# Second expert products two steps behind the first, a third gelu buffer, and a small GpSimd write behind each gather and scatter

## What is computed

```python
logits = -dist2 + jnp.einsum('bld,ed->ble', x, rw) + rb
topv, topi = jax.lax.top_k(logits, TOP_K)
w = jax.nn.softmax(topv, axis=-1)
hidden = jax.nn.gelu(jnp.einsum('bld,efd->blef', x, w1) + b1, approximate=False)
exp_out = jnp.einsum('blef,edf->bled', hidden, w2) + b2
sel = jnp.take_along_axis(exp_out, topi[..., None], axis=2)
fused = jnp.sum(w[..., None] * sel, axis=2)
```

## Time and profile before

| what | value |
|---|---|
| median of 3 runs | 615.46 us (615.41 to 619.34) |
| span of the profiled execution | 666.4 us |
| PE, DVE, ACT, POOL busy in it | 79%, 55%, 53%, 42% |
| the loop over the steps in it | about 237 to 637 us |
| share of PE in the chain that ended last | 57% |

### The profile page before, as it was taken

The page is one execution under the profiler, slowest core; times in us unless marked ns, Lnnn a source line. Parts: engine busy times, 40 slices in busy tenths (PEclk is TensorE's granted clock), DMA queues, the critical chain, the costliest instruction groups (busy, mean ns, idle before and its releaser), DMA issues.

```text
span 666.4 us, 19936 instructions
## 1 busy us (share of the span) xinstructions
PE 525.1 (79%) x6242; PEld 467.0 (70%) x6242; DVE 364.4 (55%) x1325; ACT 351.7 (53%) x1079; POOL 278.4 (42%) x308
## 2 busy tenths in 40 slices
PE   4999889997241588998888987888978888788984
PEld 4957779996030267897778876877877777777832
DVE  6564769997999734655656741112245443333126
ACT  5624156774864364556557864445545455445513
POOL 4000000000262265656666665666656566665410
PEclk9999969999575599999999999899999999999988
DMA  7980000003200355555555755555777755565463
GB/s 227 244 313 21 3 2 1 0 0 127 126 2 0 125 146 162 153 151 150 156 148 145 234 146 148 143 158 146 210 223 227 215 150 147 156 190 163 146 221 111
DMA packets 55746, 92.28 MB, mean 138 GB/s; under 512 B 10352, under 2 KB 26096, under 8 KB 55152
## 3 DMA queue, kind: packets, MB, share of 16 engines
q1 hardware_dynamic: 45424, 72.35, 36.2%
q0 software_dynamic: 10240, 18.89, 9.7%
HBM read 78.07 MB, written 17.37 MB: 143 GB/s over the span
## 4 chain that ended last, share of the span: by engine, by line
PE 57%; DVE 20%; issue 10%; ACT 6%; DVEq 3%; DMA 2%; another core or an unknown queue 1%; POOL 0%; SPq 0%; POOLq 0%; ACTq 0%
PE bank L2154 22%; PE bank L2147 18%; DVE shared L1193 2%; DVE shared L1185 2%; PE bank L2139 2%; DVEq L1669 2%; DVE early L1473 2%; ACT value L889 2%; PE bank L1741 2%; DVE early L1669 2%; DMA shared<-yd 2%; PE bank L1846 1%; PE bank L1778 1%; PE bank L2095 1%; PE bank L1768 1%
## 5 line engine op out<-in xcount | busy, mean ns | idle before, releaser
L889 ACT ACTIVATE value<-bank,shared 128x128 f32<-128x128 f32 x632 | 180.3, 380 | 181.2 <-PE bank L2147 165.6
L2154 PE MATMUL bank<-shared,value 128*128 x1264 | 177.1, 283 | 53.5 <-issue 25.5
L2154 PEld LDWEIGHTS bank<-shared,value 128*128 128x128 f32 x1264 | 154.1, 192 | 72.9 <-issue 72.2
L2147 PE MATMUL bank<-early,shared 128*128 x1264 | 173.0, 280 | 3.1 <-ACT early L897 1.9
L597 POOL DMA_INDIRECT shared<-xd,early x128 | 124.8, 975 | 87.7 <-PE bank L2147 45.5
L606 POOL DMA_INDIRECT yd<-early x128 | 126.2, 986 | 82.9 <-PE bank L2147 41.5
L2147 PEld LDWEIGHTS bank<-early,shared 128*128 128x128 f32 x1264 | 154.4, 192 | 7.0 <-issue 6.1
L1669 DVE SCALAR_TENSOR_TENSOR early<-bank,value,early 128x128 f32 x158 | 55.4, 351 | 188.9 <-PE bank L2154 115.5
L560 POOL TENSOR_TENSOR shared<-shared,xn 128x512 f32<-128x512 f32 x4 | 5.1, 1266 | 174.4 <-DVE xn L1268 166.6
L2009 PE MATMUL bank<-ksp,shared 128*128 128x32 bf16 x1536 | 41.1, 177 | 0.0
L2009 PEld LDWEIGHTS bank<-ksp,shared 128*128 128x128 bf16 x1536 | 40.2, 97 | 0.1
(11 more groups left out here) (334 smaller groups left out, 684.6 us busy)
## 6 DMA issues: line engine op xcount, KB each, us to landing
shared<-w1b SPq DMA_DIRECT2D x158, 258.0 KB
w1b<-in_w_t SPq DMA_DIRECT2D x1, 4096.0 KB, 17.4
shared<-col_dram SPq DMA_DIRECT2D x1, 4096.0 KB, 13.0
shared<-in_w_t SPq DMA_DIRECT2D x1, 4096.0 KB, 12.4
att<-yd SPq DMA_DIRECT2D x8, 512.0 KB
shared<-yd SPq DMA_DIRECT2D x4, 1024.0 KB, 9.0
xd<-xnT SPq DMA_DIRECT2D x2, 1280.0 KB
shared<-xd,early POOLq DMA_INDIRECT x128
```

The source lines that it names most:

```text
L889: ins = act.activation(hT[:, i % 2, tok(c)], bank[2 + i % 2][:, tok(c)], ACT.Gelu, bias=w1_now[:, i % WR, F + c:F + c + 1])
L2147: ins = mm(bank[2 + i % 2][:, tok(c)], w1_now[:, i % WR, tok(c)], x_now, start=True, stop=True)
L2154: ins = mm(bank[6 + i % 2][:, 0:D], hT[:, i % 2, tok(c)], w2_sb[:, bass.ds(e, 1), c, :] .rearrange("p a d -> p (a d)"), start=(c == 0), st ...
```

## The change

PE's `down` goes from one to two steps behind `up`, `hT` has HD = 3 buffers instead of 2, `gelu(j)` waits for `down(j - 3)`, and DVE's `y_add` goes from two to three steps behind. After the loop PE has two `down` left instead of one, and DVE three adds instead of two. POOL issues a memset of 128 x 64 float32 behind every gather and scatter, 256 in all, into one of four unused buffers of SBUF; from the fifth on it waits for the memset four before it, its own. The number of PSUM banks, the pacing of POOL and all DMAs stay.

```diff
+    HD = 3
...
-        hT = of_work(2 * F).rearrange("p (a f) -> p a f", a=2)
+        spare = of_work(2 * D).rearrange("p (a d) -> p a d", a=4)
+        hT = of_work(HD * F).rearrange("p (a f) -> p a f", a=HD)
...
             moved = [0]
+            first = steps[0]
+
+            def space():
+                n = steps[0] - first
+                freed(pool, const_step, steps[0] + 1 - 4 if n >= 4 else 0)
+                steps[0] += 1
+                pool.memset(spare[:, n % 4, :], 0.0).then_inc(const_step, 1)
...
                     .then_inc(xg_in[n % XSEM], 16)
+                space()
...
                                         in_=yg[:, m % SLOTS, :], in_offset=None).then_inc(y_out[m % RING], 16)
+                space()
...
             def gelu(i):
                 act.wait_ge(up_ps, i + 1)
-                freed(act, down_ps, i - 1)
+                freed(act, down_ps, i - HD + 1)
...
-                e = expert(dve, i - 2) if i >= 2 else None
+                e = expert(dve, i - HD) if i >= HD else None
...
-                if i >= 2:
-                    y_add(i - 2, e)
+                if i >= HD:
+                    y_add(i - HD, e)
...
-                if i >= 1:
-                    down(i - 1, before)
+                if i >= HD - 1:
+                    down(i - HD + 1, last)
...
+            down(IALL - 2, before)
             down(IALL - 1, e)
```

More of the change, by code:

```diff
@@ L886, in gelu @@
                 act.wait_ge(up_ps, i + 1)
-                freed(act, down_ps, i - 1)
+                freed(act, down_ps, i - HD + 1)
                 for c in range(FC):
-                    ins = act.activation(hT[:, i % 2, tok(c)], bank[2 + i % 2][:, tok(c)], ACT.Gelu,
+                    ins = act.activation(hT[:, i % HD, tok(c)], bank[2 + i % 2][:, tok(c)], ACT.Gelu,
                                          bias=w1_now[:, i % WR, F + c:F + c + 1])
@@ L1677, in _ @@
             for i in range(IALL):
-                if i - 2 == NI:
+                if i - HD == NI:
                     dve.wait_ge(exp_ready, 2)
-                e = expert(dve, i - 2) if i >= 2 else None
+                e = expert(dve, i - HD) if i >= HD else None
                 for g in range(brought(i) // GRP, brought(i + 1) // GRP):
                     bring(g)
-                if i >= 2:
-                    y_add(i - 2, e)
+                if i >= HD:
+                    y_add(i - HD, e)
                 if i < NI:
@@ L1688, in _ @@
                     finish(i)
-            for i in (IALL - 2, IALL - 1):
+            for i in range(IALL - HD, IALL):
                 y_add(i, expert(dve, i))
@@ L2153, in down @@
                 for c in range(FC):
-                    ins = mm(bank[6 + i % 2][:, 0:D], hT[:, i % 2, tok(c)], w2_sb[:, bass.ds(e, 1), c, :]
+                    ins = mm(bank[6 + i % 2][:, 0:D], hT[:, i % HD, tok(c)], w2_sb[:, bass.ds(e, 1), c, :]
                              .rearrange("p a d -> p (a d)"), start=(c == 0), stop=(c == FC - 1))
@@ L2162, in _ @@
             pe.wait_ge(gT_ready, 5)
-            before, e, after_e = None, None, expert(pe, 0)
+            last, before, e, after_e = None, None, None, expert(pe, 0)
             for i in range(IALL):
-                before, e = e, after_e
+                last, before, e = before, e, after_e
                 up(i, e)
```

## The result

The changed kernel has a median of 619.20 us over 20 runs (615.82 to 623.35), the kernel before in the same job one of 614.28 us over 20 (610.75 to 619.34). The ratio is 1.0091 [1.0066, 1.0115], with the 95% interval in brackets: slower by 0.9%, clear of the noise, though less than the 1% within which the prediction counted a time as unchanged. The forecast was 600.0. A ratio leaves out the few runs that lie over 1.5% above the fastest of their kernel, and it is not the plain quotient of the two medians, from which it differs by up to 0.3%.

A forecast was written before the change was run, and what follows sets the result against it. PE was taken to bound the loop, with 52.8 us of waits to win; POOL, at 380.8 against 407.0 us, would then bound it. The 26 us won there, weighed to 15 in the median, gave 600 us, range 570 to 638.

The forecast's parts named there:

- PE sets the loop: Expert loop: PE busy 341.92 of 400 us, the busiest other engine POOL 243.97, so PE bounds it with 58 us idle.
- the 52.8 us: PE's waits ahead of the second product in the profiled execution, 25.5 + 16.5 + 10.8 us, the most a perfect order could win.
- the lateness is mostly the profile's own: Second reading within the 0.22 rival: late announcements belong mostly to the profile, which would explain runs 50.9 us shorter.
- Announcements come late while POOL issues back to back: PE's signals release ACT, DVE and POOL late beside indirect DMAs 0.30 us apart, promptly where they stand 0.82 to 0.90 apart.
- The order: Second products and adds one step later on PE and DVE: alone wins about half of 42 us of waits, an estimated 20.
- What is late next is the add: PE's second product still needs DVE's add of two steps before, so of 0.65 us idle only about 0.35 would go.
- The price of a write: Each memset on POOL's queue costs 0.15 us, from a range of 0 to 0.45; 256 of them cost 38.4 us.
- DVE's zeroing and POOL's port: DVE's 32 zeroings of 0.485 us might lock POOL out of a shared port, delaying 4% of writes: 3 us more.
- POOL's cover: POOL's 66.2 us of waiting for first products, 0.26 us for each DMA, is what writes may cost before POOL sets the loop.
- From the profile to the median: 26 us won in the profile become 24 won or 3 lost in the runs; the first weighed twice gives 15 us.
- The writes do not part enough: Rival, chance 0.22: DMAs stay too close or the lateness is the profile's; adds still hold second products; 610 to 620 us.
- POOL is priced out: Rival, chance 0.28: writes overfill POOL's queue, from 0.26 or 0.14 us a write; 637 us at 0.35, 660 at 0.45.

The follow-up runs named there:

- the usual execution: The profiled execution of the kernel before, run again with no edit: 614.78 us, like the timed runs, whose median was 614.61 us, ratio 0.9961.

## Why the prediction was wrong, point by point

- **PE sets the loop**: held, and more than it said. In the usual execution PE is busy in 330.71 of 347 us. The step that failed is the carrying over of one execution's waits to the runs: the 52.8 us that "a perfect order could win in the profiled execution" were scaled to the median ("If all parts shrink alike, 26 x 615.46 / 666.4 = 24 us are won"). They were true of that execution only, whose span lay 50.9 us over the median; in a usual one 8.5 us stand ahead of the second product, 0.4 of them for a gelu. The prediction saw the gap, and named the reading that was right ("the lateness is mostly the profile's own, which would explain why the runs are 50.9 us shorter") as part of a rival at 0.22. What made PE's announcements late in that one execution, no run here has shown again.
- **Announcements come late while POOL issues back to back**: fell. Profiled again, POOL's DMAs start 1.29 apart for most of the loop and one gelu of 158 is over 1 us late. Two places of one trace were a correlation, as was said, and the forecast rested on it all the same; all 158 steps of that trace do not bear it out. Two of the forecast's signs came true, under 25 us ahead of the second product and prompt gelus, but both hold in before as well, so they were no success of the change.
- **The order**: "What is late next is the add" was right; of any size it was the only thing late already. The estimate of 20 us from it goes with the 42 us of gelu waits, of which 0.4 are left.
- **The price of a write**: 0.15 was taken from a range of 0 to 0.45, and 0.025 was measured. The duration was right (0.166), but the 0.30 behind a DMA shrinks to some 0.16 when a write stands there, so that most of the write costs nothing. The Trainium skill (GPSIMD Engine Reference, Instruction dispatch) would have brought the price down to 0.1; the trace goes further in that direction than the estimate from it.
- **DVE's zeroing and POOL's port**: 12 of the 256 writes overlap one of the zeroings, six of them for their whole length; these 12 last 0.165 to 0.170 us and start with the end of their DMA, as the others do. All writes of the changed kernel, shortest, median and longest in ns:

```profile
L594 POOL MEMSET value<- x256: 161/165/181, 230.7 to 586.3; 128x64 f32 x128
```

  So the lock that the Trainium skill describes for a two-port mode (SBUF — State Buffer, Who interferes with whom) shows in no row of this kernel: a write that had waited for the 485 ns of a zeroing would stand out. Whether the zeroing runs in such a mode at all, no row tells. The prediction gave it 3 us and hardly let it count, which was right.
- **POOL's cover**: 66.2 us were worked out. (The last DMA of that execution ends at 637.63, one later than the last of the earlier trace rows, so POOL's stretch was 408.6 us and not 407.0; nothing hangs on it.) By the same working the usual execution has 111.4 idle, less 13.0 ahead of the first DMA, 76.5 behind the DMAs and 9.6 for adds: 12 us. The writes (6 us) fit that as a sum, but it was the wrong sum to make: the waits lie at a few places, and from DMA 120 to 240 POOL has hardly any. There the writes are not covered, and POOL's DMAs come later and later, up to 2.9 us. That the slack of the scatters takes most of this in before, and no longer does when the adds come a step later, is a reading of the chain and the table; no run took the slack alone away.
- **From the profile to the median**: two ways were weighed, 24 us won and 3 us lost, the first twice. The second, in which the loop's share of the 50.9 us is all waiting, was the nearer one; the loop of the usual execution is in fact 56.6 us shorter, more than the 30.6 that it took. That its 3 us lost lie near the 4.9 measured is luck: it set 38.4 us of writes against 35.6 of cover, where 6 and 12 were found.
- **The rivals**: "The writes do not part enough" (610 to 620) holds the measured 619.2, by its second reason; but the order did not win its few us, and POOL's cover did not pay for the writes everywhere. "POOL is priced out" was to begin at 0.14 us a write; the kernel is slower at 0.025 and by 31 us at 0.182, so its place, POOL's queue, fits the runs, and its threshold, made from an average cover, does not. The sign "the prediction is wrong if the median lies above 609" came true.

## What to carry to other kernels

When the profiled execution is 8% longer than the timed runs, its waits need not be the kernel's: what is to be won is bounded by the runs (a stretch of 347 us with 331 of PE's work cannot give 42), and a wait that a change is to remove should be seen in an execution of the usual length first. An engine's cover is not its idle time over the whole loop but the least that it has in any stretch: where a queue runs back to back, even 0.025 us an instruction adds up, until something downstream that had been just in time is late. Two parts that each cost nothing that can be measured may cost something together; here they seem to draw on the same slack.

## What the runs showed that had not been expected

- A 128 x 64 memset of 0.166 us behind an indirect DMA moves the next one by only 0.025 us, since the idle time between them falls from 0.30 before the change to 0.15 to 0.17 behind the write. A memset of 128 x 256 (0.328 us) moves it by 0.182.
- One execution of the kernel before had its loop stretched from 342.1 to 398.7 us at the same granted clock of 1.00, with gelus that started 0.99 us after their product on average in place of 0.05. None of the twelve other profiles shows it, and its cause is open.
